# Two of POOL's four gathers moved to the head of its step in the key-value stage

## The reference, cut to what matters

```python
out = silu(xf @ sw1) * (xf @ sw3) @ sw2
out = out.at[token_idx].add(routed_out)        # two routed rows a token
x = _layernorm(x + out)                        # first norm of the stage, result x2
h = _layernorm(x, ln_w, ln_b)                  # second norm
qkv = h @ W_in + b_in
Q, K, V = jnp.split(qkv, 3, axis=-1)
Q = _rope_half(Q)
K = _rope_half(K)
A = jnp.sum(_cos_sim(K) * V, axis=-2)          # K / |K|, summed over all tokens
```

## Time and profile before

| what | us |
|---|---|
| median of three runs | 2623.27 |
| lowest and highest of them | 2622.34, 2633.66 |
| the profiled execution, its own time | 2637.1 |
| its span | 2635.4 |
| busy in the span: PE, DVE, ACT, POOL | 2167.8, 1930.7, 1554.7, 1482.8 |
| first gather of the stage to last addition to A | 2123.14 to 2339.25 |

### The profile page before, as it was taken

The page is one execution under the profiler, slowest core; times in us unless marked ns, Lnnn a source line. Parts: engine busy times, 40 slices in busy tenths (PEclk is TensorE's granted clock), DMA queues, the critical chain, the costliest instruction groups (busy, mean ns, idle before and its releaser), DMA issues. The chain is left out here.

```text
span 2635.4 us, 60664 instructions
## 1 busy us (share of the span) xinstructions
PE 2167.8 (82%) x19761; PEld 1606.0 (61%) x19761; DVE 1930.7 (73%) x5247; ACT 1554.7 (59%) x3130; POOL 1482.8 (56%) x2287
## 2 busy tenths in 40 slices
PE   8946888888887888888888699788599947768887
PEld 5634665666555566556655488666355535558887
DVE  4538999999999999999999644466333347757776
ACT  5658988888889998998988222256122212222222
POOL 2447877777778887887877323244111144424444
PEclk9977888788889988887988699888799978889999
DMA  5766666666666666666666357444222233321110
GB/s 173 244 193 181 163 161 175 163 166 164 164 172 168 179 174 165 163 179 164 169 171 154 108 169 240 160 140 142 79 84 84 77 108 121 120 73 37 48 48 28
DMA packets 295159, 373.68 MB, mean 142 GB/s; under 512 B 44628, under 2 KB 234646, under 8 KB 294902
## 3 DMA queue, kind: packets, MB, share of 16 engines
q1 hardware_dynamic: 285030, 343.10, 47.1%
q0 software_dynamic: 9872, 27.28, 3.2%
HBM read 151.03 MB, written 85.00 MB: 90 GB/s over the span
## 5 line engine op out<-in xcount | busy, mean ns | idle before, releaser
L667 POOL TENSOR_TENSOR p_CR<-p_pc 128x256 f32<-128x256 f32 x512 | 373.3, 729 | 202.9 <-DVE p_pc L991 179.4
L748 PE MATMUL p_ps_sc<-p_CR,p_BR 64*128 64x128 f32 x4096 | 352.7, 320 | 50.8 <-DVE p_M L1004 29.0
L671 POOL TENSOR_TENSOR p_BR<-p_pb 128x256 f32<-128x256 f32 x512 | 373.4, 729 | 26.1
L748 PEld LDWEIGHTS p_ps_sc<-p_CR,p_BR 64*128 64x128 f32 x4096 | 300.0, 220 | 111.2 <-issue 84.2
L881 ACT ACTIVATE p_D<-p_ps_x 128x512 f32<-128x512 f32 x512 | 289.8, 593 | 118.8 <-PE p_ps_x L714 118.0
L1004 DVE TENSOR_TENSOR p_M<-p_ps_sc,p_D 128x512 f32<-128x512 f32 x512 | 327.6, 681 | 35.5 <-PE p_ps_sc L748 35.3
L991 DVE SCALAR_TENSOR_TENSOR p_pc<-p_ps_c,p_beta,p_cs 128x256 f32<-128x256 f32 x512 | 243.4, 475 | 59.0 <-DMA p_sn<-p_tr_s 34.1
L763 PE MATMUL p_ps_y<-p_M,p_uexp 128*32 128x128 f32 x4096 | 253.0, 278 | 0.0
L991 DVE SCALAR_TENSOR_TENSOR p_pc<-p_ps_c,p_beta,p_sn 128x256 f32<-128x256 f32 x512 | 242.9, 474 | 0.0
L997 DVE SCALAR_TENSOR_TENSOR p_pb<-p_ps_b,p_beta,p_cs 128x256 f32<-128x256 f32 x512 | 242.9, 474 | 0.0
L997 DVE SCALAR_TENSOR_TENSOR p_pb<-p_ps_b,p_beta,p_sn 128x256 f32<-128x256 f32 x512 | 242.9, 474 | 0.0
(11 more groups left out here) (280 smaller groups left out, 5240.1 us busy)
## 6 DMA issues: line engine op xcount, KB each, us to landing
p_cs<-p_tr_c SPq DMA_DIRECT2D x256, 256.0 KB, 4.2
p_sn<-p_tr_s SPq DMA_DIRECT2D x256, 256.0 KB, 4.5
p_phib<-scratch_phi SPq DMA_DIRECT2D x256, 128.0 KB, 3.1
p_x<-scratch_rt SPq DMA_DIRECT2D x72, 128.0 KB, 2.0
scratch_ro<-p_o POOLq DMA_DIRECT2D x72, 128.0 KB, 2.0
p_xT<-in_xT SPq DMA_DIRECT2D x64, 128.0 KB, 4.6
scratch_u<-p_u SPq DMA_DIRECT2D x16, 512.0 KB, 3.6
scratch_wu<-p_wu SPq DMA_DIRECT2D x16, 512.0 KB, 4.3
```

What stands on the lines that cost most here:

```text
L667: e.tensor_tensor(CR[:, p, g, :], pc[:, g % 2, 0, :], pc[:, g % 2, 1, :], ALU.add).then_inc(S["rotC"], 1)
L671: e.tensor_tensor(BR[:, p, g, :], pb[:, g % 2, 0, :], pb[:, g % 2, 1, :], ALU.add).then_inc(S["rotB"], 1)
L748: m = e.matmul(sc_ps[half][:, (g * 2 + b) * L:(g * 2 + b + 1) * L], BR[half * 64:half * 64 + 64, p, 2 * q + g, b * L:(b + 1) * L], CR[half ...
```

## The change

`gather` takes the sequence b as an argument and issues two gathers instead of four. The two of b = 0 stand at the head of POOL's step, with the two waits; the two of b = 1 stand where all four stood, between the first and the second root, without a wait of their own. The prologue, which gathers for chunks 0 and 1, issues the same eight in the same order.

```diff
-            def gather(t, p):
-                e.wait_ge(S["slot_in"][1 if t >= 2 else 0], 16)
-                at_least(e, S["s2_ok"], t, 1, -1)
-                for b in range(BATCH):
-                    for n in range(2):
-                        e.indirect_dma_start(got[:, p, b, n, :], None, W["ro"].rearrange("j p d -> (j p) d"),
...
+            def gather(t, p, b):
+                if b == 0:
+                    e.wait_ge(S["slot_in"][1 if t >= 2 else 0], 16)
+                    at_least(e, S["s2_ok"], t, 1, -1)
+                for n in range(2):
+                    e.indirect_dma_start(got[:, p, b, n, :], None, W["ro"].rearrange("j p d -> (j p) d"),
...
             def step(t, p):
+                if t + 2 < NC:
+                    gather(t + 2, p, 0)
                 if t:
                     key_norm(t - 1)
                 if t + 1 < NC:
                     norm_pool(e, S2, N2, t + 1, mhalf)
                 if t + 2 < NC:
-                    gather(t + 2, p)
+                    gather(t + 2, p, 1)
                 if t + 1 < NC:
                     norm_pool(e, S, N, t + 1, mhalf)
             for t in range(2):
-                gather(t, t)
+                for b in range(BATCH):
+                    gather(t, t, b)
```

More of the change, by code:

```diff
@@ L2067, in _ @@
             e.wait_ge(S["prep"], 1)
-            def gather(t, p):
-                e.wait_ge(S["slot_in"][1 if t >= 2 else 0], 16)
-                at_least(e, S["s2_ok"], t, 1, -1)
-                for b in range(BATCH):
-                    for n in range(2):
-                        e.indirect_dma_start(got[:, p, b, n, :], None, W["ro"].rearrange("j p d -> (j p) d"),
-                                             bass.IndirectOffsetOnAxis(ap=slot[:, t, 2 * b + n:2 * b + n + 1], axis=0)
-                                             ).then_inc(S["got"][p], 16)
+            def gather(t, p, b):
[4 more added lines that the diff above has]
+                    e.indirect_dma_start(got[:, p, b, n, :], None, W["ro"].rearrange("j p d -> (j p) d"),
+                                         bass.IndirectOffsetOnAxis(ap=slot[:, t, 2 * b + n:2 * b + n + 1], axis=0)
+                                         ).then_inc(S["got"][p], 16)
             def key_norm(t):
```

## The result

| what | before | after |
|---|---|---|
| median | 2623.23 us (7 runs) | 2591.97 us (7 runs) |
| lowest and highest | 2616.30, 2633.66 | 2583.67, 2604.27 |
| ratio after/before, 95% interval | | 0.9884 [0.9854, 0.9914] |
| span of the profiled execution | 2635.4 | 2587.4 |
| stage, start of POOL's memset of A to start of the last addition to A | 218.6 | 190.8 |

The change is faster by 31.3 us (22.6 to 38.3 by the interval), where 14.3 were forecast, and lies outside the range given (2602 to 2620). The two profiled executions differ by 48 us, which is not the gain: the stage begins at 2120.65 in one and at 2099.53 in the other, behind the same code, and such differences come and go between executions. In the repetition further down the stage of the change begins at 2121.45. What the change did is inside the stage: 218.6 - 190.8 = 27.8 us, and 13 x (12.71 - 10.51) = 28.6 of its steps.

A forecast was written before the change was run, and what follows sets the result against it. POOL's lump of key norm, roots and four gathers was taken to bound each 12.71 us step. The new step's terms summed to 11.61 us, so 13 x 1.10 = 14.3 us off 2623.27 gave 2609.0 us, range 2602 to 2620.

The forecast's parts named there:

- Point 2: On POOL, from the end of DVE's addition L2200 to the first head gather: 0.08 to 0.25 us, taken as 0.20.
- (d): Rival, more gain than forecast: hand-over 0.08 us, no contention, step 11.29 us, gain 18.5 us, time 2604.8; chance 0.12.
- Points 3 to 7: From first head gather to hn: 2.29 (pair), 0.20 (contention), 0.66 and 0.86 (key norm, first root), 2.29 (pair), 0.84 us.
- about 0.5: Sign expected in the profile: DVE's idle time before hn falls from 2.4 to about 0.5 us a step.
- Point 4: Loss of both head gathers beside the queries' rotation on DVE: 0 to 0.42 us each, 0.20 in all.
- Point 6: Third and fourth gather to second root, 2.29 us; POOL stays later than DVE's variance, by 0.2 us.
- (a): Rival, small gain: fourth gather lands 0.5 us late or head gathers lose 0.42 each; about 2616 us; chance 0.25.
- a margin of 4.66 us: From the fourth gather's start to the addition L2197 that needs it landed; a landing of 4.6 us just fitted.
- (b): Rival: old steps were shorter in the median runs, 12.29 us; gain 8.8 us, time 2614.5; chance 0.12.
- (c): Rival, slower: head gathers held by DVE's whole run of SBUF operations; step 13.65 us, time 2635.5; chance 0.06.
- The 620 and 3100 ns: Skill page's times, alone and beside VectorE copies, cited as a case of an operation held by DVE.

The follow-up runs named there:

- e1: The change, but the head gathers wait one count longer of s2_ok, for their own step's addition; 12.27 us a step, ratio to before 0.9968.
- e5: The change, but one gather at the head and three between the roots; 11.15 us a step, 2600.39 us in one run.
- e6: As e1, but the head gathers wait for DVE's two statistics behind the addition; 13.08 us in most steps, 2630.04 us in one run.
- e7: As e1, but the head gathers wait for the first of DVE's two additions; 11.43 us in most steps, 2614.26 us in one run.
- e4b: The change, with the queries' last addition moved from DVE to POOL, behind the next step's head gathers; 11.08 us a step, 2607.26 us in one run.
- e9: As e8, with the addition to A and one product of the keys' rotation moved ahead of hn on DVE; 10.18 us a step, ratio to before 0.9884.
- e2: The change, but all four gathers at the head, none between the roots; 10.47 us a step, ratio to before 0.9906.
- e3: The change, but the two head gathers stand behind the key norm instead of ahead of it; 12.40 us a step, 2624.71 us in one run.
- e8: As e2, with the queries' last addition moved from DVE to POOL between the roots; 10.07 us a step, ratio to before 0.9880.

## Why the prediction was wrong

**What bounds the kernel: right.** The lump of POOL's work between squares and second root was the bound, and the step of 12.71 us was the right thing to count. What the prediction left out is that a part of this step came from TensorE's clock; the last section has it.

**Point 2, the step that failed: "they start as soon as DVE has finished the addition L2200".** That is a misreading of one count in the code, not of the trace. The call is `gather(t + 2, p, 0)`, and its wait `at_least(e, S["s2_ok"], t, 1, -1)` has the fetched chunk as t. So it wants t + 1 additions in terms of POOL's step t, those of chunks 0 to t, and DVE makes the last of these in its step t - 1. The addition of the same step makes chunk t+1's sums, and its buffer is the other one. The wait was met long ago; the gathers start 0.9 us behind the start of the previous second root. The section on the kernel before says that a gather waits until the addition has read its buffer; the prediction then took the wrong addition, which reads the other buffer. e1 is the kernel with the wait that I had priced, and the 1.76 us a step between it and the change are the price of the mistake.

Worked out after the result, with the right count, the same rows come near it. Both head gathers fit into POOL's idle time before the key norm, so between the squares and hn only two gathers are left. By e5's list POOL would need 10.98 - 1.26 = 9.72 us for a step, and DVE's own run is longer. DVE had 28.7 us of idle time in 12 steps, 2.4 a step, so the step could fall to 12.71 - 2.4 plus the wait that stays for the hand-over: 10.3 to 10.5, and with 10.5 the gain is 13 x 2.2 = 28.6 us and the time 2594.7. Neither the forecast nor a rival had that case: (d), "more than forecast", stopped at 11.29 a step.

**Point 2's size.** Even for e1 it was 0.59 us short: 0.79 instead of 0.20. The bounds 0.08 and 0.25 came from a root behind DVE and a gather behind a root, and neither is a gather behind another engine. They should have been called no upper bound at all. The two errors of point 2 have opposite signs; priced rightly, the kernel that I had in mind gains 13 x 0.44 = 5.7 us, less than half of the forecast.

**Points 3 to 7: right for the kernel they describe.** e1 has each within 0.05 us, and its 0.51 us of idle time before hn is the "about 0.5" of the prediction's signs. Point 4, the loss of the second gather beside the rotation, was taken as 0.20, and it is 0.22 (1.19 against 0.97).

**Point 6, who is late at the second root,** was 0.2 us from tipping over, and did so as soon as point 2 fell: in the change the root waits 0.77 us for the variance.

**Rivals.** (a) did not show: in the change no row has L2200 (the first addition after the change) waiting for a gather past the prologue. The fourth gather starts at 2219.71 and that addition at 2225.13, 5.4 us later, and in the repetition of the change no landing of these steps took over 4.5 us. The prediction was still right to worry about a margin of 4.66 us, as e5 shows. (b) can't be settled from one trace of the kernel before, but the two gains in the medians, 31.3 and 26.9 us (2633.19 - 2606.28), lie on both sides of the 28.6 us of the steps, not below them. Its remark that the new step doesn't hang on the squares is borne out. (c), the hold by DVE's run, is refuted by e6 and e7. It was the page "SBUF — State Buffer" of the Trainium skill that this rival leant on. What its section "Who interferes with whom" says of two-input operations agrees with e4b, where DVE's two grew from 0.49 and 0.76 to 1.07 and 1.17 us beside an addition on POOL; a gather beside such operations took at most some 0.5 us more (1.49 against 0.95, in the prologue of the change; 1.47 in most steps of e9). The 620 and 3100 ns that the prediction cites stand on that page under "A bandwidth-pool intuition that's wrong (but worth ruling out)", not in the box on blocked DMA, and are for a VectorE `tensor_copy`. No run here puts a gather beside such a copy. That what a gather loses beside a two-input addition is a wait for the lock, as the prediction took it, is not shown either: it lost 0.1 us where 0.27 us of the addition were left (e2), and 0.42 where 0.55 were left.

## What to carry to other kernels

Before pricing an instruction that is moved ahead of a wait, write out in numbers what its own wait asks for (which chunk, which buffer, which step of the other engine), since one count decides whether it lands in the idle time or behind it. Work that an in-order engine does in one lump while it also idles should go into the idle time; splitting it elsewhere brings little (0.31 us a step in e3, against 2.20). And once the lump is gone, look which engine's own run is the floor: here DVE's, which e8 shows by shortening it.

## What the runs showed of the hardware that I had not expected

A gather that waits for DVE starts 0.78 to 0.79 us behind the release, at three different releases (e1, e6, e7), where POOL's root starts 0.08 us behind DVE's variance, and a gather behind an instruction of POOL 0.17 us behind it. That the gather's start-up is hidden behind POOL's running instruction in the last case would explain all three, but is only argued.

The granted clock of TensorE was higher where its idle times were shorter. The windows of the steps before and after, with PE, PEld, DVE, ACT and POOL busy, then the granted clock, DMA share and GB/s:

```profile
2161.00:2314.00 153.00, 117.19 (x480) 87.08 (x480) 118.20 (x409) 43.27 (x132) 73.54 (x84) 0.90 0.40 123
```

```profile
2138.00:2264.00 126.00, 104.59 (x480) 77.29 (x480) 117.90 (x408) 42.29 (x132) 74.53 (x84) 1.00 0.52 151
```

The same 12 chunks cost PE 117.19 us before and 104.59 after. Before, the turning started behind 2.1 to 3.3 us of idle time, about 3 us in most steps, and stretches of the lower level (1.2 GHz) made the mean 0.90; after, PE is idle for 1.5 to 1.9 us there and the clock stays at 2.4 GHz throughout. That the shorter idle time is what kept the clock up is argued, not shown: no run changes it by itself.

What the clock cost can be read from the steps. The same view of two neighbouring steps of the kernel before:

```profile
2186.59:2198.84 12.25, 8.72 (x40) 6.44 (x40) 9.83 (x35) 3.52 (x11) 6.11 (x7) 1.00 0.46 138
2198.84:2212.06 13.22, 10.03 (x40) 7.64 (x40) 9.82 (x34) 3.63 (x11) 6.13 (x7) 0.87 0.42 135
```

and of one step of e1:

```profile
2194.49:2206.78 12.29, 10.46 (x40) 7.77 (x40) 9.92 (x35) 3.64 (x11) 6.33 (x7) 0.80 0.41 128
```

Before, the four of the 13 steps with a clock of 1.00 took 12.18 to 12.26 us, the nine at 0.86 and 0.87 took 12.29 to 13.24. PE's work was in the loop, by way of the squares for which the key norm waited. In e1, where POOL's gathers are over later than the squares, ten of the 13 steps take 12.28 to 12.30 us at clocks from 0.79 to 1.00. After the change the squares come in time as well: 11 of 13 steps take 10.48 to 10.50 us. So of the 2.20 us that the mean step lost, an estimate of 0.48 (12.71 less the 12.23 of the four steps at 1.00) goes with the clock, and 1.72 with the order of POOL's work. The same estimate says that e1, the kernel that the prediction had in mind, gains its 0.44 us only because its step doesn't lengthen with the clock: it is no shorter than an old step at 1.00.
